# Graph layer with residual norm: every fourth pair of x turned on VectorE, features numbered 4p+k

## What is computed

```python
msg = x[src]
agg = jax.ops.segment_sum(msg, dst, num_segments=n)
deg = jax.ops.segment_sum(jnp.ones((src.shape[0],), x.dtype), dst, num_segments=n)
mean = agg / jnp.maximum(deg, 1.0)[:, None]
h = mean @ W_l + b + x @ W_r
out = _layernorm(x + h * jax.nn.sigmoid(h), axis=-1)
```

## Time and profile before

| what | us |
|---|---|
| median of the runs | 1617.12 |
| the profiled execution | 1616.76 |
| its span | 1615.0 |
| TensorE busy | 1574.8 (98%) |
| VectorE busy | 1408.7 (87%) |
| ScalarE busy | 1028.8 (64%) |
| POOL busy | 947.9 (59%) |

### The profile page before, as it was taken

One profiled execution on the slowest core, in us unless ns is written; L12 is line 12 of the kernel. 1 busy time (PEld: TensorE's weight loads), 2 busy tenths in 40 slices (PEclk: granted clock), 3 DMA queues, 4 the chain that ended last, 5 costly groups with the idle time before them and its releaser, 6 DMA issues.

```text
span 1615.0 us, 24709 instructions
## 1 busy us (share of the span) xinstructions
PE 1574.8 (98%) x7886; PEld 1311.1 (81%) x7886; DVE 1408.7 (87%) x2174; ACT 1028.8 (64%) x1433; POOL 947.9 (59%) x1089
## 2 busy tenths in 40 slices
PE   7998899999999999999999999999999999999996
PEld 5887688888888888888888888888888888888884
DVE  7988799999996888888888888888888888888886
ACT  4443343333335777777777777777777777777775
POOL 6446566666654665655566556665556656666563
PEclk9999999999999999999999999999999999999998
DMA  5456589888884676766667666666667666677674
GB/s 186 147 163 189 170 262 266 263 265 262 266 250 150 220 230 201 237 211 216 223 208 227 218 213 219 219 221 213 222 212 228 217 210 231 205 228 221 205 235 152
DMA packets 204245, 350.52 MB, mean 217 GB/s; under 512 B 37020, under 2 KB 51126, under 8 KB 204117
## 3 DMA queue, kind: packets, MB, share of 16 engines
q1 hardware_dynamic: 156135, 274.22, 51.6%
q0 software_dynamic: 46944, 74.22, 16.7%
q10 hardware_dynamic: 1038, 0.50, 0.1%
HBM read 288.78 MB, written 139.67 MB: 265 GB/s over the span
## 4 chain that ended last, share of the span: by engine, by line
PE 95%; DVE 2%; DMA 1%; issue 1%; SPq 0%; ACT 0%; POOL 0%; POOLq 0%; DVEq 0%
PE pH L473 81%; PE pT L567 9%; PE pT L541 3%; PE pT L482 1%; DMA light_h<-in_x 0%; DVE w_sum L799 0%; DVE w_sum L794 0%; DVE sums L923 0%; DMA light_x<-in_x 0%; PE pH L500 0%; PE pH L503 0%; DVE stats L1001 0%; SPq L246 0%; DVE row_mask L790 0%; DVE Z L794 0%
## 5 line engine op out<-in xcount | busy, mean ns | idle before, releaser
L473 PE MATMUL pH<-ws_hi,x_hi 128*128 128x512 f32 x1564 | 629.1, 402 | 0.0
L473 PE MATMUL pH<-ws_hi,x_lo 128*128 128x512 f32 x1564 | 611.4, 391 | 0.0
L473 PE MATMUL pH<-ws_lo,x_hi 128*128 128x512 f32 x1564 | 609.4, 390 | 0.0
L383 POOL DMA_INDIRECT cor<-correction_rows,node_idx x347 | 366.2, 1055 | 313.3 <-ACT cor L671 229.8
L708 ACT ACTIVATE x_hi<-pT 128x1024 fp32r<-128x1024 f32 x174 | 178.1, 1024 | 272.7 <-PE pT L567 272.7
L473 PEld LDWEIGHTS pH<-ws_hi,x_lo 128*128 128x128 f32 x1564 | 293.6, 188 | 63.3
L473 PEld LDWEIGHTS pH<-ws_lo,x_hi 128*128 128x128 f32 x1564 | 294.7, 188 | 54.5
L473 PEld LDWEIGHTS pH<-ws_hi,x_hi 128*128 128x128 f32 x1564 | 294.2, 188 | 54.5 <-issue 0.3
L986 DVE TENSOR_TENSOR Z<-pH,cor 128x1024 f32<-128x1024 f32 x174 | 212.5, 1221 | 100.4 <-PE pH L473 94.6
L717 ACT ACTIVATE O<-Z,shift,rstd 128x512 f32<-128x512 f32 x347 | 261.9, 804 | 3.2 <-DVE shift L1011 3.2
L1001 DVE BATCH_NORM_STATS2 stats<-Z 128x6 f32<-128x512 f32 x347 | 221.4, 680 | 0.0
(11 more groups left out here) (132 smaller groups left out, 1785.6 us busy)
## 6 DMA issues: line engine op xcount, KB each, us to landing
X<-in_x SPq DMA_DIRECT2D x173, 512.0 KB, 4.2
out<-O SPq DMA_DIRECT2D x173, 512.0 KB, 5.1
correction_rows<-c_out SPq DMA_DIRECT2D x98, 256.0 KB, 4.2
light_x<-in_x SPq DMA_DIRECT2D x66, 256.0 KB, 5.0
light_h<-early_product SPq DMA_DIRECT2D x44, 256.0 KB, 5.7
out<-light_o SPq DMA_DIRECT2D x44, 256.0 KB, 5.5
join_row<-joined SPq DMA_DIRECT2D x98, 64.0 KB, 4.1
light_h<-in_x SPq DMA_DIRECT2D x22, 256.0 KB, 2.9
```

Source lines behind the costliest of these rows:

```text
L383: g.indirect_dma_start(out=out_, out_offset=None, in_=table, in_offset=bass.IndirectOffsetOnAxis(ap=idx, axis=0), bounds_check=bound, oob_ ...
L473: last = mm(ps, a[:, k], w[:, k], start=(n == 0), stop=(n == len(terms) - 1))
```

## The change

Three things, which belong together.

The features of a chunk are numbered anew: chunk k holds the features 4p + k, p = 0 to 127. The weights are loaded so (partition p of chunk k takes row 4p + k), and each transpose on TensorE reads every fourth column of its rows, through the new `features`. The order within x_hi and x_lo becomes chunk, tile, row, so that a chunk's 128 rows still stand side by side.

Every fourth pair (`by_blocks`: t mod 4 = 3, below the last pair) is not transposed by TensorE. `load_blocks` loads its x a second time, in eight DMAs: block (i, j), 32 rows by 128 columns, goes to partitions 32j to 32j + 31. VectorE's 32x32 transpose (`turn_blocks`, 1024 elements per partition) makes x_blocks of it in one instruction, two pairs ahead; ScalarE's rounding and VectorE's x_lo then read x_blocks in SBUF instead of pT. X itself is still loaded for the residual sum. The buffers are the four xs tiles of the edge stage, free by then.

The semaphore `transposed` is counted without these pairs (`pe_turned`), and `blocks_in`, `blocks_turned` are new. The changed lines of the early stage's x_hi and of xs, which only follow the new shapes, are left out here.

```diff
         X = sb("X", [P, 4, 2, D], f32)
-        x_hi = [sb(f"x_hi{b}", [P, 2, K, P], f32r) for b in range(2)]
-        x_lo = [sb(f"x_lo{b}", [P, 2, K, P], f32r) for b in range(2)]
+        x_hi = [sb(f"x_hi{b}", [P, K, 2, P], f32r) for b in range(2)]
+        x_lo = [sb(f"x_lo{b}", [P, K, 2, P], f32r) for b in range(2)]
         cor = [sb(f"cor{b}", [P, 2, D], f32) for b in range(4)]
...
         dst_f = sb("dst_f", [P, 1 + ET], f32)
         rdeg = sb("rdeg", [P, ET], f32)
-        xs = [sb(f"xs{b}", [P, D], f32) for b in range(4)]
+        xs = sb("xs", [P, 4, D], f32)
+        x_raw, x_blocks = xs[:, 0:2], xs[:, 2:4]
         xd = [sb(f"xd{b}", [P, D], f32) for b in range(4)]
...
         x_in = [sem(f"x_in{b}") for b in range(4)]
         cor_in = [sem(f"cor_in{b}") for b in range(4)]
+        blocks_in, blocks_turned = sem("blocks_in"), sem("blocks_turned")
         transposed, hi_made, lo_made, product, z_made, silu_made = (sem("transposed"), sem("hi_made"), sem("lo_made"),
...
         block = ctx.enter_context(nc.Block())
+        def features(rows, k):
+            return rows.rearrange("p (m k) -> p k m", k=K)[:, k]
+
         def fixed(v):
...
             return u % n, q * (4 // n) + u // n
+
+        def by_blocks(t):
+            return t % 4 == 3 and t < NP - 1
+
+        def pe_turned(t):
+            return t + 1 - (t + 1) // 4
+
+        def in_blocks(tile):
+            return tile[:].rearrange("p k a (i r) -> p (a i) k r", r=32)
...
             single(0, load_early)
             for k in range(K):
-                sp.dma_start(wl_raw[:, k], w_l[k * P:(k + 1) * P, :]).then_inc(weights_in[k], 16)
-                sp.dma_start(wr_raw[:, k], w_r[k * P:(k + 1) * P, :]).then_inc(weights_in[k], 16)
+                sp.dma_start(wl_raw[:, k], w_l.rearrange("(p k) n -> k p n", k=K)[k]).then_inc(weights_in[k], 16)
+                sp.dma_start(wr_raw[:, k], w_r.rearrange("(p k) n -> k p n", k=K)[k]).then_inc(weights_in[k], 16)
             single(1, load_early)
...
                     sp.dma_start(X[0:rows, b, 0], x[BASE + t * 2 * P:N, :]).then_inc(x_in[b], 16)
+            def load_blocks(t):
+                if t == 3:
+                    sp.wait_ge(diff_made, ET)
+                wait(sp, blocks_turned, (t + 1) // 4 - 1)
+                for a in range(2):
+                    first = BASE + (2 * t + a) * P
+                    for j in range(4):
+                        sp.dma_start(x_raw[32 * j:32 * j + 32, a].rearrange("r (i c) -> r i c", i=4),
+                                     x[first:first + P, j * P:(j + 1) * P].rearrange("(i r) c -> r i c", r=32)
+                                     ).then_inc(blocks_in, 16)
+
             def store_out(t, q, u):
...
             def move(t, q, u):
                 shifted(t, q, u, 3, NP, load_x)
+                if by_blocks(t + 4):
+                    load_blocks(t + 4)
                 shifted(t, q, u, -3, NP, store_out)
                 light(q, u)
+            load_blocks(3)
             peeled(0, NP, move)
...
                 wait(pe, early_copied, t - 1)
                 for k in range(K):
-                    last = nc.tensor.transpose(pT[b][:, 0, k * P:(k + 1) * P], e_x[b][:, k * P:(k + 1) * P], eye)
+                    last = nc.tensor.transpose(pT[b][:, 0, k * P:(k + 1) * P], features(e_x[b][:], k), eye)
                 last.then_inc(early_transposed, 1)
...
                 wait(pe, sums_made, t - 1)
                 for k in range(K):
-                    last = nc.tensor.transpose(runs[b][:, k * RUN + 2:(k + 1) * RUN], diff[b][:, k * P:(k + 1) * P],
+                    last = nc.tensor.transpose(runs[b][:, k * RUN + 2:(k + 1) * RUN], features(diff[b][:], k),
                                                eye)
...
             def transpose_x(t, q, u):
+                if by_blocks(t):
+                    return
                 nt, rows = pair_shape(t)
...
                     for k in range(K):
                         last = nc.tensor.transpose(pT[u % 2][:, a, k * P:k * P + rows],
-                                                   X[0:rows, b, a, k * P:(k + 1) * P], eye[0:rows, 0:rows])
+                                                   features(X[0:rows, b, a], k), eye[0:rows, 0:rows])
                 last.then_inc(transposed, 1)
...
                 wait(pe, z_made, t - 1)
                 for a in range(nt):
-                    last = three(pH[b][0:rows, a, :], x_hi[b][:, a, :, 0:rows], x_lo[b][:, a, :, 0:rows],
+                    last = three(pH[b][0:rows, a, :], x_hi[b][:, :, a, 0:rows], x_lo[b][:, :, a, 0:rows],
                                  ws_hi, ws_lo)
...
                 nt, rows = pair_shape(t)
                 b = u % 2
-                wait(act, transposed, t + 1)
                 wait(act, product, t - 1)
-                a_(x_hi[b][:, 0:nt, :, 0:rows],
-                   pT[b][:, 0:nt].rearrange("p a (k r) -> p a k r", k=K)[:, :, :, 0:rows], ACT.Copy).then_inc(hi_made, 1)
+                if by_blocks(t):
+                    act.wait_ge(blocks_turned, (t + 1) // 4)
+                    a_(in_blocks(x_hi[b]), x_blocks.rearrange("p a (i k r) -> p (a i) k r", k=K, r=32), ACT.Copy
+                       ).then_inc(hi_made, 1)
+                else:
+                    act.wait_ge(transposed, pe_turned(t))
+                    a_(x_hi[b][:, :, 0:nt, 0:rows].rearrange("p k a r -> p a k r"),
+                       pT[b][:, 0:nt].rearrange("p a (k r) -> p a k r", k=K)[:, :, :, 0:rows], ACT.Copy
+                       ).then_inc(hi_made, 1)
...
                 b = u % 2
                 wait(dve, hi_made, t + 1)
-                v.tensor_tensor(x_lo[b][:, 0:nt, :, 0:rows],
-                                pT[b][:, 0:nt].rearrange("p a (k r) -> p a k r", k=K)[:, :, :, 0:rows],
-                                x_hi[b][:, 0:nt, :, 0:rows].bitcast(f32), ALU.subtract).then_inc(lo_made, 1)
+                if by_blocks(t):
+                    v.tensor_tensor(in_blocks(x_lo[b]), x_blocks.rearrange("p a (i k r) -> p (a i) k r", k=K, r=32),
+                                    in_blocks(x_hi[b]).bitcast(f32), ALU.subtract).then_inc(lo_made, 1)
+                else:
+                    v.tensor_tensor(x_lo[b][:, :, 0:nt, 0:rows].rearrange("p k a r -> p a k r"),
+                                    pT[b][:, 0:nt].rearrange("p a (k r) -> p a k r", k=K)[:, :, :, 0:rows],
+                                    x_hi[b][:, :, 0:nt, 0:rows].rearrange("p k a r -> p a k r").bitcast(f32),
+                                    ALU.subtract).then_inc(lo_made, 1)
+
+            def turn_blocks(t, q, u):
+                dve.wait_ge(blocks_in, 128 * ((t + 1) // 4))
+                if t >= 7:
+                    wait(dve, lo_made, t - 3)
+                v.transpose(x_blocks.rearrange("p a (i k r) -> p (a i) k r", k=K, r=32),
+                            x_raw.rearrange("p a (i c k) -> p (a i) k c", i=K, k=K)).then_inc(blocks_turned, 1)
...
                 shifted(t, q, u, -1, NP, residual)
                 shifted(t, q, u, -2, NP, make_shift)
+                if by_blocks(t + 2):
+                    single(t + 2, turn_blocks)
                 light(q, u)
```

More of the change, by code:

```diff
@@ L365, in split_early @@
                 wait(pool, early_done, t - 1)
-                g.tensor_tensor(x_lo[b][:, 0], e_t[b][:].rearrange("p (k r) -> p k r", k=K),
-                                x_hi[b][:, 0].bitcast(f32), ALU.subtract).then_inc(early_lo, 1)
+                g.tensor_tensor(x_lo[b][:, :, 0], e_t[b][:].rearrange("p (k r) -> p k r", k=K),
+                                x_hi[b][:, :, 0].bitcast(f32), ALU.subtract).then_inc(early_lo, 1)
             peeled(0, 4, split_early)
@@ L392, in gather_xs @@
             def gather_xs(t, q, u):
-                gather(xs[u][:], x, src_idx[:, t:t + 1], P, N - 1, xs_in[u])
+                gather(xs[:, u], x, src_idx[:, t:t + 1], P, N - 1, xs_in[u])
             pool.wait_ge(dst_found, 1)
@@ L490, in early_tile @@
                 wait(pe, early_kept, t - 1)
-                three(pH[0][:, b, :], x_hi[b][:, 0], x_lo[b][:, 0], ws_hi, ws_lo,
+                three(pH[0][:, b, :], x_hi[b][:, :, 0], x_lo[b][:, :, 0], ws_hi, ws_lo,
                       ws_split if fixed(t) and t == 0 else None).then_inc(early_done, 1)
@@ L620, in round_early @@
                 wait(act, early_done, t - 1)
-                a_(x_hi[b][:, 0], pT[b][:, 0, :].rearrange("p (k r) -> p k r", k=K), ACT.Copy).then_inc(early_hi, 1)
+                a_(x_hi[b][:, :, 0], pT[b][:, 0, :].rearrange("p (k r) -> p k r", k=K), ACT.Copy).then_inc(early_hi, 1)
                 wait(act, early_lo, t - 1)
@@ L912, in subtract @@
                 wait(dve, turned, t - 1)
-                v.tensor_tensor(diff[b][:], xs[r][:], xd[r][:], ALU.subtract).then_inc(diff_made, 1)
+                v.tensor_tensor(diff[b][:], xs[:, r], xd[r][:], ALU.subtract).then_inc(diff_made, 1)
             def scan(t, q, u):
```

## The result

The changed kernel takes 1667.82 us (median of 4 runs, 1665.41 to 1668.70) against 1616.78 for the kernel before: a ratio of 1.0313, 95% interval 1.0297 to 1.0328, 51 us slower. The prediction said 1580 us and faster. The profiled execution took 1665.41 us (span 1663.6).

What follows compares the result with a forecast made beforehand. TensorE, with its transposes in the path, was taken as the bound: 1616.8 - 37.4 us for transposes removed, all other terms 0 or hidden, gave 1579.4, on the median's scale 1579.8, said as 1580 us; range 1576 to 1742.

Steps and rivals of the forecast that it cites:

- its cost is 0, hidden by TensorE's products: VectorE's transpose in every fourth pair: costs 0 behind TensorE's products; without that cover 43 x 1.24 = 53 us.
- VectorE's transpose: Pairs t = 1 mod 4: 1.24 us per instruction, from a cast of the same size; range 0.69 to 2.7.
- the 23.3 us of the prediction: VectorE's time in four pairs, 22.0 + 1.24 us, against TensorE's 24.49: 95% busy.
- the step of four on TensorE: All remaining transposes read every fourth column: taken at 0, with an upper end of 160 us.
- the gap of those that went: 43 pairs lose 8 transposes of 0.87 us each, products following directly: 37.4 us leave TensorE's path.
- The block loads: Eight extra 64 KB DMAs on SP per four pairs, 3.5 us to issue, hidden: cost 0.
- the bound of 0.119 us per load: Upper price of a stepped weight load on TensorE: 1343 loads, 160 us, 1739 us in all; chance 0.37.
- the 0.028: Price in us per stepped weight load on TensorE from which 1343 loads cost the 37.4 us gain.
- its estimate of 1726 us: TensorE's stepped loads at half rate, one hit per 16-byte line: 0.109 us more per counted load.
- Rival 3: VectorE becomes the bound: at 2.7 us per transpose 1589 us, up to 1606 with waits for POOL's rstd; chance 0.08.
- those waits shrink when VectorE is late: Argument against VectorE as bound: its waits for POOL's rstd, 28.0 us in 40 times, would get shorter.
- 0.03 x 43 = 1.3 us: VectorE's x_lo in 43 pairs, reading SBUF instead of PSUM: 1.22 against 1.19 us each, hidden.

Runs made afterwards that it cites:

- e2_tiny_turn: The changed kernel with VectorE's transpose cut to one 32x32 block, loads, step and waits kept: 1600.15 us, ratio 0.9898.
- e5_one_load: The changed kernel with the eight block loads done once only, ahead of the node stage: 1666.73 us, ratio 1.0295.
- e4_dense_turn: The changed kernel with VectorE's transpose reading 32 neighbouring elements at a time instead of every fourth: 1633.98 us, ratio 1.0101.
- e12_step_two_late_shift: The changed kernel with VectorE's shift one step later, features numbered for a step of two elements, and sixteen block loads of 256-byte pieces: 1685.63 us, ratio 1.0408.
- e7_xlo_psum: The changed kernel with x_lo of block pairs reading the PSUM tile pT instead of x_blocks in SBUF: 1602.89 us, ratio 0.9901.
- e3_rstd_first: The changed kernel with POOL making the pair's rstd ahead of the gathers, the light rstd staying behind them: 1774.81 us, ratio 1.0981.
- e9_late_shift: The changed kernel with VectorE's pair shift and light shift each taken one step later, POOL's order unchanged: 1614.42 us, ratio 0.9982.
- e13_step_two_merged: The changed kernel with the later shift and a step of two elements, its sixteen block loads joined to eight covering both tiles: 1597.48 us, ratio 0.9871.

## Why the prediction was wrong, step by step

The step that failed is "its cost is 0, hidden by TensorE's products". VectorE's transpose took 2.02 us in place of 1.24, and VectorE's waits for POOL, which the 23.3 us of the prediction leave out, came to 2.29 us in four pairs: VectorE needed 26.10 us where TensorE needs 24.84. Beside it the step of four on TensorE, taken at 0, cost 25.9 us.

**Right.** The bound before was TensorE with its transposes in the path, and the gap of those that went closes: 48 matmuls stand in one piece in e2_tiny_turn. The block loads cost nothing (e5_one_load, e2_tiny_turn). ScalarE's rounding of block pairs takes 1061 ns against 1001 and stays hidden. TensorE's share of the sum, with its measured prices, comes out: 1616.8 - 43 x 0.96 + 25.9 = 1601.4, and e2_tiny_turn, which leaves VectorE out, took 1600.15.

**The step of four on TensorE**, taken at 0, costs 25.9 us. I chose the lower end because the transposes' own rows were "nearest"; the bound of 0.119 us per load held, and 0.019 lies a sixth of the way up. It is two thirds of the 0.028 at which it would eat the whole gain. With this alone the forecast would have been 1601 us and still faster. The prediction's sentence from the Trainium skill on lines of 16 bytes was right that this step isn't free, but its estimate of 1726 us, from half rate, was far off.

**VectorE's transpose**, taken at 1.24 us, took 2.02. The row that I chose is exact for the transpose without a step (1.238 in e4_dense_turn). The prediction discussed the step of four at length for TensorE and did not see that the same numbering puts it into VectorE's read as well. Here the rule of lines (the Trainium skill, SBUF — State Buffer, "Door 1: The DMA port swizzle") fits: with two hits on a line (e12_step_two_late_shift) 1.24 us, with one 2.02.

**"Its cost is 0, hidden"** failed by more than the size of the term. With 2.02 us VectorE has 23.81 us of work in four pairs, still less than TensorE's 3 x 0.96 + 4 x 5.49 = 24.84. What tipped it are 2.29 us of waits for POOL. The prediction's 23.3 us were work alone; the waits for the light rstd in the earlier trace rows, 28.0 us in 1000, are 0.7 us in four pairs on top. Rival 3 had this place but set the price at 9 to 26 us, with the sentence that "those waits shrink when VectorE is late". They don't: POOL's rstd begins with VectorE's mv and is wanted by VectorE's shift in the same step, so a late VectorE makes POOL late by as much. l_shift waits 26.6 us (28.0 before), and the shift's wait grew from 5.3 to 60.5.

**"0.03 x 43 = 1.3 us" for x_lo out of SBUF** was right for VectorE (1192 ns) and missed the price that it puts on another engine: 65 us (e7_xlo_psum), nearly all that VectorE's lateness costs. That price stood in the trace of before, behind the very wait for the light rstd in the earlier trace rows. There l_var_eps, the same operation as var_eps on one number per partition, falls beside the residual of line 993, which reads two operands in SBUF:

```profile
1010.70 1.22 DVE L993 TENSOR_TENSOR Z<-Z,X 128x1024 f32<-128x1024 f32 x1
...
1012.69 0.16 DVE L1034 SCALAR_TENSOR_TENSOR l_shift<-l_mv,l_rstd 128x1 f32<-128x1 f32 x1 [0.70 <-POOL l_rstd L428]
```

```profile
1010.79 1.21 POOL L426 TENSOR_SCALAR l_var_eps<-l_mv 128x1 f32<-128x1 f32 x1
```

It takes 1.21 us, 1121 ns in the mean over the kernel, and l_shift waits 0.70 us. In e3_rstd_first, where the gathers move l_var_eps away from the residual, it takes 247:

```profile
L454 POOL TENSOR_SCALAR l_var_eps<-l_mv 128x1 f32<-128x1 f32 x44 | 10.9, 247 | 1.5 <-DVE l_mv L1077 0.3
```

How little room the pair's own rstd had is in the trace of before too, in the step whose x_lo is the one of the earlier trace rows:

```profile
1003.64 0.24 POOL L442 TENSOR_SCALAR var_eps<-mv 128x2 f32<-128x2 f32 x1
1003.97 0.73 POOL L445 TENSOR_TENSOR rstd<-var_eps,minus_half 128x2 f32<-128x2 f32 x1
...
1005.50 0.15 DVE L1011 SCALAR_TENSOR_TENSOR shift<-mv,rstd 128x2 f32<-128x2 f32 x1
```

rstd was ready at 1004.70 and wanted at 1005.50: 0.8 us of room, and a var_eps of 1.09 or 1.28 us in place of 0.24 uses it up.

**The sum of the causes.** 1616.8 + 25.9 (step on TensorE) - 41.3 (transposes gone) = 1601.4; the kernel after stands 68 us above e2_tiny_turn's 1600.15, and these are VectorE's. They don't split into parts that add up: dense reading gives back 34, the late shift 53, the one operand 65, together over twice the 68. It takes both, the longer work and POOL's delay: without the transpose (e2_tiny_turn) or without the operand's price (e7_xlo_psum) alone the kernel is within 3 us of TensorE's 1600, and from there on a further saving on VectorE can give little.

**Left open.** Why eight stepped transposes take 0.96 and not 0.87 us: a step of two elements costs TensorE nearly the same (0.95), which the Trainium skill's rule of two hits on a line doesn't explain. And the last 14 us of e9_late_shift, whose chain still goes through POOL and VectorE: no run took them apart, but with the step of two (e13_step_two_merged) they are gone.

## What to carry to other kernels

A wait between two engines inside one step doesn't shrink when the whole step gets late; ask for each cross-engine pair how much room it has (here 0.8 us) and what runs beside the helper. When an operand moves from PSUM to SBUF, cost it on the neighbour that shares the memory, not only on the engine that reads it. When a layout changes, write down every instruction that reads with the new step, on each engine, and look for a smaller step: here two elements instead of four, the result taken one step later and the loads kept to eight turned 3% slower into 1.3% faster.

## What the runs showed of the hardware

- VectorE's 32x32 transpose of 128 x 1024 fp32 takes 1.24 us with a step of 4 or 8 bytes and 2.02 us with a step of 16.
- TensorE's stepped transposes take 0.95 to 0.96 us per eight at a step of 8 as of 16 bytes, 0.87 without.
- GpSimd's var_eps, a TENSOR_SCALAR on 2 elements per partition, takes 0.22 to 0.24 us beside a VectorE instruction with one operand in SBUF, and 1.09 to 1.28 beside one of 1.2 us with two. rstd, a TENSOR_TENSOR of that size, takes 0.72 and 1.56.
- Sixteen block loads on SP take 8.66 us to issue, eight of twice the size 4.58: the same bytes in the same pieces, and 88 us of the kernel's time between them (a granted clock of 0.98 against 1.00 included).
